# An attention and mixture-of-experts layer in one software pipeline: combine weights spread by DMA and applied on GpSimd, values scaled in two steps, one piece for the output projection

## What is computed

```python
x = x + attention(layernorm(x))      # 16 heads, 16 key and 64 value columns each
x = x + experts(layernorm(x))

# attention, per block and head
q, k, v = l2norm(q), l2norm(k), l2norm(v)
aggr = square(relu(q @ k.T)) @ v
out = tanh(|aggr|) * aggr/|aggr| * tanh(silu(gates))
out @ Wout

# experts, per token: 4 of 16 are chosen, in 2 of 4 groups
combine = top4(masked sigmoid scores), normalised, * 2.5       # 256 x 16 per block
y = sum_e combine[:, e] * ((silu(x @ w_gate[e]) * (x @ w_up[e])) @ w_down[e])
y + shared expert (the same form, 128 columns, no weight)
```

## Time and profile before

| | us |
|---|---|
| median of 3 runs | 753.18 |
| the profiled execution | 755.62 |
| its span, first to last instruction | 753.6 |
| PE busy | 680.0 |
| DVE, ACT, POOL busy | 543.5, 431.8, 354.3 |
| mean granted clock of TensorE, of full speed | 0.971 |

### The profile page before, as it was taken

How to read it: one execution, slowest core, us unless ns; L and a number is a source line. 1 busy time by engine, 2 the same in 40 slices (tenths; PEclk the granted TensorE clock), 3 DMA queues, 4 the chain that set the end, 5 groups by cost and what they waited for, 6 DMA issues and landing times.

```text
span 753.6 us, 15281 instructions
## 1 busy us (share of the span) xinstructions
PE 680.0 (90%) x5160; PEld 525.0 (70%) x5160; DVE 543.5 (72%) x1739; ACT 431.8 (57%) x986; POOL 354.3 (47%) x368
## 2 busy tenths in 40 slices
PE   3676898999999999999999999999999999998876
PEld 2544476777777777777777777777777777666775
DVE  4555558687887968687877968686878868686653
ACT  4575666656665675656666675756566656453211
POOL 3245565554646464554555463645546464643000
PEclk9887999999999999999999999999999999999789
DMA  9994949394654829191845739190927548000000
GB/s 265 112 142 58 137 57 127 39 139 52 119 72 93 97 69 113 31 141 29 131 59 106 85 79 106 64 117 18 152 33 118 66 91 92 2 15 2 8 7 8
DMA packets 72829, 61.24 MB, mean 81 GB/s; under 512 B 8624, under 2 KB 72496, under 8 KB 72752
## 3 DMA queue, kind: packets, MB, share of 16 engines
q1 hardware_dynamic: 72752, 60.26, 54.8%
HBM read 41.37 MB, written 18.87 MB: 80 GB/s over the span
## 4 chain that ended last, share of the span: by engine, by line
PE 48%; DVE 29%; ACT 12%; issue 9%; DMA 1%; POOL 1%; DVEq 0%; SPq 0%; ACTq 0%; POOLq 0%
PE ps_f L440 9%; PE ps_f L421 8%; PE ps_a L499 7%; PE ps_f L358 6%; PE ps_f L360 4%; PE ps_f L359 4%; DVE it L855 4%; DVE norms_y L663 3%; ACT sq L565 3%; DVE norms_t L662 3%; PE ps_s L467 3%; PE ps_f L400 3%; ACT v L562 2%; ACT r L601 2%; DVE it L872 2%
## 5 line engine op out<-in xcount | busy, mean ns | idle before, releaser
L326 POOL TENSOR_TENSOR p<-r 128x512 f32<-128x512 f32 x256 | 263.8, 1051 | 316.0 <-ACT r L601 283.2
L601 ACT ACTIVATE r<-ps_s 128x512 f32<-128x512 f32 x256 | 141.8, 618 | 84.0 <-PE ps_s L467 79.7
L499 PE MATMUL ps_a<-p,v 128*64 128x256 f32 x1024 | 146.2, 397 | 3.0 <-DVE big L901 1.6
L499 PEld LDWEIGHTS ps_a<-p,v 128*64 128x64 f32 x1024 | 64.5, 137 | 43.3 <-POOL p L326 4.8
L593 ACT ACTIVATE it<-ps_f 128x256 f32<-128x256 f32 x144 | 55.5, 385 | 64.4 <-PE ps_f L360 61.3
L901 DVE TENSOR_TENSOR big<-ps_a,wt 128x256 f32<-128x256 f32 x128 | 53.6, 420 | 39.6 <-ACT big L610 38.5
L855 DVE TENSOR_TENSOR it<-ps_f,it 128x256 f32<-128x256 f32 x144 | 58.9, 419 | 29.4 <-ACT it L593 28.8
L440 PE MATMUL ps_f<-wdown,it 128*128 128x128 f32 x576 | 71.3, 285 | 3.3 <-DVE it L872 3.3
L440 PEld LDWEIGHTS ps_f<-wdown,it 128*128 128x128 f32 x576 | 68.7, 199 | 4.3 <-DVE it L872 4.3
L467 PE MATMUL ps_s<-qkt 64*128 64x256 f32 x512 | 66.0, 333 | 3.4 <-ACT r L601 1.9
L344 POOL TENSOR_TENSOR v<-v,vs 128x512 f32<-128x512 f32 x64 | 66.6, 1042 | 3.4 <-DVE vs L778 3.4
(11 more groups left out here) (153 smaller groups left out, 1524.5 us busy)
## 6 DMA issues: line engine op xcount, KB each, us to landing
qk_rows<-qk_parts SPq DMA_DIRECT2D x16, 1024.0 KB, 4.7
qkt<-qk_rows SPq DMA_DIRECT2D x64, 256.0 KB, 10.0
qkt<-qk_rows SPq DMA_DIRECT2D x128, 128.0 KB, 9.4
x_in<-in_L_attn_tokens SPq DMA_DIRECT2D x16, 128.0 KB, 2.2
x_res<-in_L_attn_tokens SPq DMA_DIRECT2D x16, 128.0 KB, 14.3
out<-o_sb SPq DMA_DIRECT2D x16, 128.0 KB, 13.4
big<-in_L_attn_Wqg SPq DMA_DIRECT2D x1, 640.0 KB, 4.1
big<-in_L_attn_Wkv SPq DMA_DIRECT2D x1, 640.0 KB, 5.4
```

Of the source, the lines that this page charges most:

```text
L326: pool.tensor_tensor(p[h % 4][:], r[h % 2][:], r[h % 2][:], ALU.mult).then_inc(probs_done, 1)
L499: last = pe.matmul(ps_a[k % 2][64 * e:64 * e + 64, 0:N], v[s % 3][:, t, h * DV:(h + 1) * DV], p[h % 4][:, t * N:(t + 1) * N], start=(t == ...
L601: act.activation(r[h % 2][:], ps_s[h % 2][:], ACT.Relu).then_inc(relu_done, 1)
```

## The change

The spreading of the combine weights leaves PE. DVE writes comb in the order that suits a flat row (two tensor_scalar in place of one product and the three operations of the split), PE transposes it into 16 partitions (cT, now in slot 2 instead of 3), ACT copies it to ct, and SyncE stores it to DRAM (c_rows) and reads it back with two DMAs, each of which broadcasts one row of 8 KB to 64 partitions of cb. GpSimd multiplies cb into `it`: j = 0 and 1 in slot 5, 2 in slot 6, 3 in slot 7, behind the squarings of the slot. The cB jobs and DVE's scale_hidden are gone.

GpSimd's value scaling takes heads 0 to 7 in slot 4 of the step before, and the last eight heads in slots 0 and 1 of the step that uses them; PE waits for them ahead of the values of slots 0 and 4. The inverse root of the second layer norm goes from slot 6 to slot 5. The two y jobs stand next to each other, x2T goes from the end of slot 7 to the end of slot 6, rT ahead of gu6, and on DVE the head scales stand in slot 2, ahead of gu4. Aggregates and gates share three buffers (heads3) in place of two pairs. The expert weights are made ready in step -1.

```diff
     [("N", "ones", 0), ("F", "gu", 0), ("P", "g", 0), ("N", "nT", 0), ("F", "gu", 1)],
-    [("F", "gu", 2), ("P", "g", 1), ("F", "gu", 3), ("F", "gu", 4)],
-    [("P", "g", 2), ("F", "gu", 5), ("F", "cT", 0), ("F", "gu", 6), ("O", "rT", 0)],
+    [("F", "gu", 2), ("F", "cT", 0), ("P", "g", 1), ("F", "gu", 3), ("F", "gu", 4)],
+    [("P", "g", 2), ("F", "gu", 5), ("O", "rT", 0), ("F", "gu", 6)],
     [("O", "rB", 0), ("O", "rB", 1), ("F", "gu", 7), ("O", "rB", 2), ("L", "xT", 0), ("O", "rB", 3), ("P", "g", 3),
      ("F", "gu", 8)],
-    [("O", "y", 0), ("L", "qk", 0), ("O", "y", 1), ("F", "cB", 0)],
-    [("L", "qk", 1), ("L", "v", 0), ("F", "cB", 1), ("L", "v", 1), SKIP],
-    [("L", "v", 2), ("F", "cB", 2), ("L", "v", 3), ("F", "cB", 3), ("O", "x2T", 0), SKIP],
+    [("O", "y", 0), ("O", "y", 1), ("L", "qk", 0)],
+    [("L", "qk", 1), ("L", "v", 0), ("L", "v", 1), ("O", "x2T", 0), SKIP],
+    [("L", "v", 2), ("L", "v", 3), SKIP],
 ]
...
 JOBS = {"xT": 1, "qk": 2, "v": 4, "g": 4, "ones": 1, "nT": 1, "rT": 1, "rB": 4, "y": 2,
-        "x2T": 1, "lg": 1, "gu": FC, "cT": 1, "cB": 4, "y2": 2}
+        "x2T": 1, "lg": 1, "gu": FC, "cT": 1, "y2": 2}
...
-    RAW = 2 * (HK + HV) + 2 * FC * P
-    big = sb("big", [P, max(RAW, 3 * NP * N)])
+    big = sb("big", [P, 4 * NP * N])
     a2 = big[:, 0:NP * N].rearrange("p (c n) -> p c n", n=N)
-    aw = [big[:, q * NP * N:(q + 1) * NP * N].rearrange("p (c n) -> p c n", n=N) for q in (1, 2)]
-    raw_experts = 3 * NP * N - 2 * FC * P
-    assert 2 * (HK + HV) <= raw_experts and 2 * NP * N - N <= raw_experts
+    heads3 = [big[:, m * NP * N:(m + 1) * NP * N].rearrange("p (c n) -> p c n", n=N) for m in (1, 2, 3)]
+    raw_experts = 4 * NP * N - 2 * FC * P
+    assert 2 * (HK + HV) <= 2 * NP * N <= raw_experts
...
+        def spread_combine(b):
+            sp.wait_ge(read["cT"], b + 1)
+            wait(sp, c_spread, 32 * b)
+            sp.dma_start(c_rows.rearrange("e (c n) -> (e c) n", n=N), ct[:]).then_inc(c_stored, 16)
+            sp.wait_ge(c_stored, 16 * b + 16)
+            wait(sp, it_scaled, 4 * b)
+            for e in range(2):
+                sp.dma_start(cb[64 * e:64 * e + 64, :, :].rearrange("p c n -> p (c n)"),
+                             c_rows[e:e + 1, :].broadcast_to([64, NP * N])).then_inc(c_spread, 16)
         def step(s, q, on, at):
...
                 sp.dma_start(x_res[q][:], tokens[s].rearrange("(t p) d -> p t d", p=P)).then_inc(x_back[q], 16)
+            if "F" in on:
+                spread_combine(s - 2)
             if "L" in on:
...
                     load_x(b + 2, q)
+            if "L" in on:
                 sp.wait_ge(read["qk"], 2 * b + 2)
...
             pool.tensor_tensor(dst[:], src[:], minus_half[:].broadcast_to([P, T]), ALU.pow).then_inc(ready, 1)
+        def scale_values(b, half, ts):
+            pool.wait_ge(vs_ready, b + 1)
+            pool.wait_ge(read["v"], 4 * b + 4)
+            for t in ts:
+                view = v[b % 3][:, t, half * 512:(half + 1) * 512].rearrange("p (h d) -> p h d", d=DV)
+                scale = vs[:, t, half * NP:(half + 1) * NP]
+                pool.tensor_tensor(view, view, broadcast(scale, [P, NP, DV], 2), ALU.mult).then_inc(v_normed, 1)
...
                     tables()
-                if k == 6 and "O" in on:
+                if "P" in on and k == 4:
+                    scale_values(s + 1, 0, (0, 1))
+                if "A" in on and k in (0, 1):
+                    scale_values(s, 1, (k,))
+                if "F" in on and k in (5, 6, 7):
+                    b = s - 2
+                    for j in ((0, 1), (2,), (3,))[k - 5]:
+                        pool.wait_ge(read["gu"], FC * b + 2 * j + 2)
+                        pool.wait_ge(c_spread, 32 * b + 32)
+                        part = it[:, 2 * j:2 * j + 2, :]
+                        pool.tensor_tensor(part, part, cb[:, 2 * j:2 * j + 2, :], ALU.mult).then_inc(it_scaled, 1)
+                if k == 5 and "O" in on:
                     pool.wait_ge(ch_n, 3 * s)
                     root(rstd2, var2, rstd2_ready)
-                if "P" in on:
-                    b = s + 1
-                    if k in (4, 5, 6, 7):
-                        t, half = divmod(k - 4, 2)
-                        pool.wait_ge(vs_ready, b + 1)
-                        pool.wait_ge(read["v"], 4 * b + k - 3)
-                        view = v[b % 3][:, t, half * 512:(half + 1) * 512].rearrange("p (h d) -> p h d", d=DV)
-                        scale = vs[:, t, half * NP:(half + 1) * NP]
-                        pool.tensor_tensor(view, view, broadcast(scale, [P, NP, DV], 2), ALU.mult)\
-                            .then_inc(v_normed, 1)
...
             else:
-                pe.wait_ge(read["cB"], 4 * b + 4)
+                pe.wait_ge(it_scaled, 4 * b + 4)
+                pe.wait_ge(read["gu"], FC * b + FC)
                 for c in range(FC):
...
                     wait(pe, aw_done, 8 * s + k - 1)
-                    if k == 0:
-                        pe.wait_ge(v_normed, 4 * s + 4)
+                    if k in (0, 4):
+                        pe.wait_ge(v_normed, 4 * s + (2 if k == 0 else 4))
                     for t in range(T):
...
                 if j == 0:
-                    wait(act, aw_done, 8 * (b - 1))
+                    wait(act, done["y"], 2 * (b - 2))
                 act.wait_ge(done[kind], count)
-                dst = wt[pq][:, 2 * j:2 * j + 2, :]
+                dst = heads3[b % 3][:, 2 * j:2 * j + 2, :]
                 act.activation(dst, ps[:].rearrange("p (c n) -> p c n", n=N), ACT.Silu).then_inc(read[kind], 1)
...
                 act.activation(n2row[:], ps[:, 0:N], ACT.Copy).then_inc(read[kind], 1)
-            elif kind in ("rT", "cT"):
-                spread, uses = (rt, "rB") if kind == "rT" else (ct, "cB")
-                wait(act, done[uses], 4 * b)
+            elif kind == "rT":
+                wait(act, done["rB"], 4 * b)
                 act.wait_ge(done[kind], count)
-                act.activation(spread[0:2 * H, :], ps[0:2 * H, 0:N], ACT.Copy).then_inc(read[kind], 1)
+                act.activation(rt[0:2 * H, :], ps[0:2 * H, 0:N], ACT.Copy).then_inc(read[kind], 1)
+            elif kind == "cT":
+                wait(act, c_stored, 16 * b)
+                act.wait_ge(done[kind], count)
+                act.activation(ct[:], ps[0:E, 0:N], ACT.Copy).then_inc(read[kind], 1)
             elif kind == "x2T":
...
                         gates(j, s, q)
-                if at == 0 and k == 5:
+                if at == -1 and k == 5:
                     expert_weights()
...
             link(dve.reciprocal(den[:], den[:]))
-            link(dve.scalar_tensor_tensor(out=comb[:], in0=chosen[:], scalar=SCALE,
-                                          in1=broadcast(den[:], [P, T, E], 2), op0=ALU.mult, op1=ALU.mult))
-            split(link, cs, comb[:], c_ready)
+            wait(dve, done["cT"], b)
+            for t in range(T):
+                last = dve.tensor_scalar(comb[:, t, :].rearrange("p (e c) -> p c e", e=2),
+                                         chosen[:, t, :].rearrange("p (c e) -> p c e", e=2),
+                                         den[:, t:t + 1], SCALE, ALU.mult, ALU.mult)
+            last.then_inc(c_ready, 1)
...
                 if ("A" in on and k > 0) or (O and k == 0):
-                    pair, ab, ap = (k - 1, s, q) if k > 0 else (NP - 1, b, pq)
+                    pair, ab = (k - 1, s) if k > 0 else (NP - 1, b)
                     dve.wait_ge(a2_done, 8 * ab + pair + 1)
                     dve.wait_ge(gate_ready, 4 * ab + pair // 2 + 1)
-                    if pair == 0:
-                        wait(dve, done["y"], 2 * (s - 1))
-                    dve.tensor_tensor(aw[ap][:, pair, :], ps_a[pair % 2][:, 0:N], wt[ap][:, pair, :], ALU.mult)\
-                       .then_inc(aw_done, 1)
+                    part = heads3[ab % 3][:, pair, :]
+                    dve.tensor_tensor(part, ps_a[pair % 2][:, 0:N], part, ALU.mult).then_inc(aw_done, 1)
...
                     if F:
-                        gate_up([3, 4])
-                if k == 3:
+                        gate_up([3])
                     if O:
...
                         link_o.end()
+                    if F:
+                        gate_up([4])
+                if k == 3:
                     gated_heads(k)
...
                     gated_heads(k)
-                    if at == 0:
+                    if at == -1:
                         expert_weights()
...
                         residual_row(0)
-                    if L_on:
-                        low_parts(0, s + 2)
-                    if O:
                         residual_row(1)
...
                         link_n.end()
-                    if F:
-                        scale_hidden([0])
+                    if L_on:
+                        low_parts(0, s + 2)
                 if k == 6:
                     gated_heads(k)
+                    if O:
```

(54 more changed lines are left out.)

9 lines of the change are left out of this document (5 added, 4 removed).

## The result

The changed kernel takes 820.41 us (median; 819.36 to 820.56) where the kernel before takes 753.28: a ratio of 1.088, 95% interval 1.0857 to 1.0908. The profiled execution has a span of 818.6 us against 753.6, which makes 65.0 us to find.

A forecast was written before the change was run, and what follows sets the result against it. Loop bound by DVE in slots 2 and 3, PE in slots 4, 0 and 1, ACT in slots 5 to 7. 13.2 + 11.6 - 4 + 1 = +21.8 on 755.62 gives 777.4, less 2.4: 775.0 us; range 755 to 792.

The forecast's parts named there:

- gu4 wait: Slot 2: PE waits 2.1 to 2.3 us at gu4 for DVE's read of gu2; net +1.15 us a step.
- slots 5 to 7: From y 0 to the router's tanh, ACT's backlog sets the time: +0.1 us a step, ends -0.4 and +0.5.
- slot 4: In slot 4 DVE is no longer late: -0.15 us a step.
- x2T late: In slots 5 to 7, x2T comes up to 2 us late, but beside ACT's backlog.
- clock: Half of 14 steps lose 1.65 us to half clock speed after gu4's wait: +11.6 us, ends 0 and +23.
- start: Expert weights move from step 0 to step -1, with a PE wait of 4.78: -4 us (0 to -5).
- tail: Last F step: path to y2 through cT, store, spread and four GpSimd multiplies: +1 us (-1 to +4).
- slices of the clock below 9: A sign that the prediction is right: granted-clock slices below 9 in the middle of the profile.
- the moved values: Value multiplies of 1.05 us moved to slots 0 and 1: cost nothing, covered by DVE's 0.87 us wait for gu1.
- rival 3: Moved value multiplies hold DVE's routing chain in full, gu1 read 0.5 us late: +7, 782 us; chance 0.08.
- rival 2: The spread lands 3 us late, holding GpSimd's slot 6 squarings, x2T and values: 800 us or more; chance 0.07.
- Rival 1: Slot 2 squarings miss the Newton steps, gu2 is read 1.45 us earlier, the clock holds: 745 us; chance 0.12.

The follow-up runs named there:

- e1: The changed kernel with cT's job one place earlier, ahead of gu2, so that it takes gu4's bank: 781.55 us, ratio 1.035.
- e3: The changed kernel with two edits of order, cT ahead of gu2 and x2T with its DVE operations back in slot 7: 758.26 us, ratio 1.0035.
- e4: The changed kernel with 14 unused matmuls of 256 columns ahead of gu4 and of x2T, from step 2 on, order unchanged: 792.49 us, ratio 1.0498.
- e2: The changed kernel with x2T and its DVE operations back at the end of slot 7: 802.91 us, ratio 1.0636.
- e5: e3 with DVE instead of GpSimd multiplying it by cb in the two steps with F but no A jobs: 752.68 us, ratio 0.9965.
- e8: e5 with the expert weights split in step 0 again instead of step -1: 751.46 us, ratio 0.9962.
- e10: e5 with gu6 ahead of rT in slot 3: 743.84 us, ratio 0.9854.
- e13: The kernel of e10 once more, on the same chip as e12: 741.9 us, ratio 0.983.
- e7: e3 with all four value multiplies back in slots 4 to 7 of the step before: 759.81 us, ratio 1.0069.
- e12: The kernel before, with only DVE's head scales moved from slot 3 to slot 2, ahead of the gated heads: 745.05 us, ratio 0.9881.

## Why the prediction was wrong

The direction and the first mechanism held; the size did not, and 820.4 lies outside the range of 755 to 792. By the profiled spans, in the prediction's own terms:

| term | predicted | measured | from |
|---|---|---|---|
| gu4 wait, slots 5 to 7, slot 4, per step | +1.10 | +1.25 | 44.16 less 41.88, less x2T |
| x2T late, per step | 0 | +1.03 | e1's step at full clock (42.55) less e3 (41.52) |
| these, times 12 | +13.2 | +27.4 | e4 against before |
| clock | +11.6 | +26.0 | 12 x 2.16 |
| start | -4 | +1.2 | 135.41 less 134.23 |
| tail | +1 | +10.4 | 127.3 less 116.9 |
| sum | +21.8 | +65.0 | |

**Slot 2 was right.** gu4 waits 2.07 or 2.53 us against 2.1 to 2.3 forecast, put down to DVE, with no wait for rs any more. That last part holds only beside gu4's wait, which makes rT come later: e3_both, without it, waits 0.43 for rs in the same order of DVE. The sign "slices of the clock below 9" did not show, since one stretch of 3.41 us at half the clock in a slice of 20.5 us leaves 0.92; the windows show the loss.

**The step that failed first is "slots 5 to 7": "This makes x2T late by up to 2 us, and that lies beside ACT's backlog."** The lateness was sized rightly, 2.07 us, though its parts were short (xn2's pair takes 2.35 beside GpSimd, not 1.97, and a hidden multiply 1.27, not 1.05); the cover was not. PE's jobs run in order, and behind x2T stand the scores and values of slot 7 and v2 and v3, on which ACT then waits in its turn. ACT's timeline in e1_cT_first, in the step at full clock:

```profile
457.62 0.39 ACT L612 ACTIVATE xn<-ps_f 128x256 f32<-128x256 f32 x1 [0.44 <-PE ps_f L451]
...
459.90 0.60 ACT L588 ACTIVATE v<-ps_f 128x512 f32<-128x512 f32 x1 [0.36 <-PE ps_f L383]
```

From its copy of qk 0 to the tanh of the router ACT takes 11.66 us in this step (451.38 to 463.04) and stands still twice, 0.80 us; in e3_both it takes 10.45 (438.44 to 448.89) and never stands still. So about half of the 2.07 was hidden; the other 1.03 is the difference between these two periods (42.55 less 41.52).

**The clock term failed on number, and little on price.** I gave half of 14 steps a drop of 1.65 us for one wait, and gave x2T's wait no chance to draw one. There were 19 drops in twelve periods, at 26.0 / 19 = 1.4 us each: 7 behind gu4's wait, as many as I had given it, and 12 behind x2T's. A wait that I had costed at nothing for its own length was never asked what it does to the clock, though the earlier trace rows had a wait of 1.81 with the lower clock behind it. In e1, x2T's wait alone draws 8 drops in twelve steps; in e2, where gu4's wait stands alone, no step is without one. So the half for gu4 was luck: by itself this wait costs 44.7 us with its clock (802.91 less e3's 758.26), and e2, which has it alone, lies above the range too. x2T's alone costs 23.3 (781.55 less 758.26); together they cost 62, less than the sum.

**Ends.** The tail cost 10.4 us instead of 1. Of these 3.8 went with the waits and their clock (127.3 to e3's 123.5) and 3.8 with the GpSimd multiplies of the last two F steps (e3 to e5, 119.7). I had named that chain rightly and priced its excess at 1 us. The remaining 2.8 stand between e5 and before; DVE's wait of 2.13 for cb in e5 may be part of it, which is not shown. These parts are rough: e5 and e8, with the same last steps, differ by 1.4 here (119.8 and 118.4), and e10 and e13, which wait 1.73 and 2.10 for cb, end 115.9 and 114.8 us behind rT of step 14. At the start, rT of step 1 did come 2.9 us earlier (92.05 against 94.97), but one step later the gain was gone: PE waited 2.60 at gu2, for DVE's read of gu0, in the first F step. e10 and e13, the same kernel, have the next rT at 136.49 and 132.22, so neither -4 nor +1.2 can be read from one profile; e8 against e5 says about 0.

**Right:** the moved values cost nothing (e7: putting them back gains nothing; rival 3 did not occur). The spread was in time: its copies are issued at 320.62, land after 5.7 us in the median, and GpSimd takes up cb at 330.52 without a wait, except in the last F step (rival 2 did not occur). Rival 1 did not occur: the Newton pieces beside squarings still take 0.94 and 0.97. By the page I named in the prediction (the Trainium skill, Perfetto Trace Analysis, "Optimizing Scalar/DVE Operations") work moved to GpSimd might not help; the runs agree so far as that e13 with the moves and e12 without them have the same period. They do not show the shared port as what cost the 65 us by itself: e3 keeps all the GpSimd work and gives 62 us back. But the hold of xn2, 2.35 us in place of 0.59, is most of what made x2T late.

## What to carry to other kernels

Price a new wait on TensorE twice: what of its length comes through, and whether it draws the lower clock; here the second was as large as the first. When a stage is called covered by another engine's backlog, list what is queued behind the late job on its own engine before costing it at zero. And before crediting a rewrite of the data path, try the cheapest reorder on the old kernel: moving four short DVE operations ahead gave 9 us, where the rewrite with all its waits mended gave 10 to 12.

## What was not expected of the hardware

- Keeping PE busy through two waits a step with 28 useless matmuls (1.81 and 1.77 us) held the granted clock at 1.00 and took 28 us off the program.
- Waits of one length, 2.07 us, at one place of the loop, were followed by 1.00 in some steps and by the lower level in others (e1: 8 stretches of lower clock in 12 steps). Waits of 0.93 (e4), 0.76 (e7) and 0.70 (before) in the twelve steps were never followed by it.
- GpSimd's product of two tiles takes 1.27 us for 128x512 (L365), the square of one tile 1.04 (L349), and DVE does the first in 0.62 (2.50 for four). The Trainium skill (GPSIMD Engine Reference, 4.1 Engine selection) gives GpSimd as about two times slower on two inputs; the 4.92 against 2.50 here agree.
